# First stage of a mixture-of-experts kernel: five channel groups of 24 rows in place of four of 32, variance by VectorE, normalisation on GpSimd inside the channel loop, x handed on per image group

## The reference, cut to what matters

```
m = mean(x, channels);  v = var(x, channels);  y = (x - m) / sqrt(v + eps)
weight[c, kh, kw] = codebook[hash(c, kh, kw)] * sign(c, kh, kw)
x1[n, c] = x[n, c] + sum over kh, kw of weight[c, kh, kw] * y[n, c, h + kh - 3, w + kw - 3] + bias[c]
```

## Time and profile before

| what | us |
|---|---|
| median of three runs | 1649.24 |
| span of the profiled execution (the page gives no other time of it) | 1726.5 |
| VectorE starts on x | 7.57 |
| first product of the convolution | 80.06 |
| last step of the convolution on VectorE | 215.06 |
| routing stage's first loads | 255.22 |
| first scatter | 273.52 |
| last scatter of the routing stage | 530.21 |

### The profile page before, as it was taken

How to read it: one execution, slowest core, us unless ns; L and a number is a source line. 1 busy time by engine, 2 the same in 40 slices (tenths; PEclk the granted TensorE clock), 3 DMA queues, 4 the chain that set the end, 5 groups by cost and what they waited for, 6 DMA issues and landing times. The chain is left out here.

```text
span 1726.5 us, 31708 instructions
## 1 busy us (share of the span) xinstructions
PE 1207.4 (70%) x6568; PEld 956.4 (55%) x6569; DVE 1106.1 (64%) x4125; ACT 587.5 (34%) x1099; POOL 699.3 (41%) x680
## 2 busy tenths in 40 slices
PE   4799903223222999999946979889797089999940
PEld 4799902212122999998934545455454067777730
DVE  7677704434345666666648688787876467777754
ACT  4233303323231444444432234334344134444320
POOL 0100005565574444444434045345554535555530
PEclk9899955555555999999976989989898589999975
DMA  4033297121111222222232011121011122222239
GB/s 200 22 107 106 64 121 273 53 58 55 39 44 46 66 62 62 62 63 60 62 128 79 1 46 51 28 58 42 26 32 31 40 73 74 75 79 71 73 103 261
DMA packets 139200, 129.26 MB, mean 75 GB/s; under 512 B 56291, under 2 KB 119012, under 8 KB 138214
## 3 DMA queue, kind: packets, MB, share of 16 engines
q1 hardware_dynamic: 89396, 79.76, 16.9%
q0 software_dynamic: 19968, 39.44, 7.0%
q10 hardware_dynamic: 29778, 9.45, 2.7%
HBM read 78.66 MB, written 50.99 MB: 75 GB/s over the span
## 5 line engine op out<-in xcount | busy, mean ns | idle before, releaser
L594 POOL DMA_INDIRECT routed<-r_xn,r_slot x320 | 333.3, 1042 | 346.6 <-DVEq L583 233.9
L823 POOL DMA_INDIRECT answers<-e_y,e_dest x304 | 291.1, 958 | 347.1 <-ACT e_y L922 272.9
L972 DVE COPY e_ht<-e_ps_ht 128x512 f32<-128x512 f32 (+1 forms) x304 | 169.5, 558 | 180.9 <-PE e_ps_ht L859 156.7
L867 PE MATMUL e_ps_y<-w,e_ht 128*128 x1824 | 258.6, 278 | 13.4 <-DVE e_ht L972 7.4
L867 PEld LDWEIGHTS e_ps_y<-w,e_ht 128*128 128x128 f32 x1824 | 228.6, 192 | 20.1 <-issue 18.8
L1135 PE MATMUL c_pz<-c_c,down 116*120 116x512 f32 (+1 forms) x392 | 199.7, 627 | 0.0
L922 ACT ACTIVATE e_y<-e_ps_y,e_weight 128x128 f32<-128x128 f32 x304 | 111.8, 368 | 217.7 <-issue 117.9
L859 PE MATMUL e_ps_ht<-ident,e_h 128*128 128x128 f32 x912 | 150.8, 274 | 6.0 <-DVE e_h L958 5.5
L849 PE MATMUL e_ps_h<-w1h,e_xl 128*128 x308 | 150.9, 490 | 1.1 <-issue 0.7
L1109 PE MATMUL c_py<-c_xh,gl 121*116 121x512 f32 (+1 forms) x196 | 124.1, 633 | 39.1 <-DVE c_xl L1215 27.1
L859 PEld LDWEIGHTS e_ps_ht<-ident,e_h 128*128 128x128 f32 x912 | 115.4, 141 | 56.0 <-DVE e_h L958 10.7
(11 more groups left out here) (134 smaller groups left out, 2445.4 us busy)
## 6 DMA issues: line engine op xcount, KB each, us to landing
e_xg<-routed SPq DMA_DIRECT2D x318, 66.0 KB
answers<-answers SPq DMA_DIRECT2D x32, 480.0 KB
c_w<-in_w SPq DMA_DIRECT2D x32, 448.0 KB
c_x<-in_xh SPq DMA_DIRECT2D x4, 1536.0 KB
routed<-r_xn,r_slot POOLq DMA_INDIRECT x320
answers<-e_y,e_dest POOLq DMA_INDIRECT x304
x<-x SPq DMA_DIRECT2D x96, 48.0 KB
w1l<-in_w SPq DMA_DIRECT2D x2, 2048.0 KB, 10.3
```

Source lines behind the costliest of these rows:

```text
L594: ro.nc.gpsimd.indirect_dma_start(ro.xs, bass.IndirectOffsetOnAxis(ap=ro.slot[0:px, q, c:c + 1], axis=0), ro.xn[0:px, q, k, t, :], None).t ...
L823: nc.gpsimd.indirect_dma_start(ys, bass.IndirectOffsetOnAxis(ap=dest[:, s:s + 1], axis=0), y[:, s, :], None).then_inc(stored[s], 16)
L867: ins = nc.tensor.matmul(ps_y[s % 2][:, 0:P], ht[:, s % 2, c * P:(c + 1) * P], wt.w2[:, bass.ds(w + c * P, P)], start=c == 0, stop=c == ch ...
L972: nc.vector.tensor_copy(ht[:, s % 2, :], ps_ht[s % 2][:, 0:HID]).then_inc(ht_ready, 1)
```

## The change

Five groups of 26 channel indices stand on 5 x 24 = 120 partitions (CP), with no blank rows; the last group has 24 real channels and two of zeros. The columns are now ordered by image group, image column and image (of four), and so are the padded buffers. The number of channel indices falls from 32 to 26. The matrices are 120 x 120.

The mean is subtracted into a buffer `cen` of the layout of x, one instruction per quarter. ScalarE squares into `sq`, which now uses the memory of `r.x`; VectorE sums the squares over the channels and one small product per quarter adds over the groups. The inversion is done once for all 384 columns. The normalisation itself is done by GpSimd for one channel at a time into a ring of three padded buffers, inside the loop. Signs and bias are applied by ScalarE on the accumulator (two instructions), and VectorE adds the result to x. Loops of this stage are written out.

The first constants of the routing stage are loaded at the start of the first one. x stays on the chip past the first stage; the routing stage stores it in four DMAs, one per image group, and loads a tile by one DMA per image row and channel group once the group's store has landed.

```diff
-CGS, CIN, RPAD = 4, 32, 32
+CGS, CIN = 5, 26
+CP = CGS * SIDE
+LAST_CIN = P - CIN * (CGS - 1)
+LAST_P = (CGS - 1) * SIDE
...
+            for i in range(CIN):
+                if i >= NRING:
+                    pool.wait_ge(split_ready, i - NRING + 1)
+                nc.gpsimd.tensor_tensor(nrm[0:CP, i % NRING, :, HALO:HALO + SIDE, :].rearrange("p g w t -> p g (w t)"),
+                                        cen[0:CP, :, i].rearrange("p (g n) -> p g n", g=IMAGE_GROUPS),
+                                        rstd[0:CP, :].rearrange("p (g n) -> p g n", g=IMAGE_GROUPS), ALU.mult).then_inc(normed, 1)
...
+            def square(q):
+                act.wait_ge(centred, q + 1)
+                nc.scalar.activation(sq[0:CP, quarter(q), 0:LAST_CIN], cen[0:CP, quarter(q), 0:LAST_CIN], ACT.Square)
+                nc.scalar.activation(sq[0:LAST_P, quarter(q), LAST_CIN:CIN], cen[0:LAST_P, quarter(q), LAST_CIN:CIN], ACT.Square
+                                     ).then_inc(squared, 1)
+
+            def high_w(i):
+                act.wait_ge(w_in[i % WRING], 16 * (i // WRING + 1))
+                if i >= 2:
+                    act.wait_ge(acc_ready, i - 1)
+                nc.scalar.activation(wh[0:CP, i % 2], wring[0:CP, i % WRING], ACT.Copy).then_inc(wh_ready, 1)
+
+            def high_x(i):
+                act.wait_ge(normed, i + 1)
+                nc.scalar.activation(ph[0:CP, i % 2], nrm[0:CP, i % NRING], ACT.Copy).then_inc(ph_ready, 1)
+
+            def scale_out(i):
+                act.wait_ge(acc_ready, i + 1)
+                acc = ps[i % 4][0:CP, 0:NW].rearrange("p (a b t) -> p a b t", b=2, t=IG)
+                for odd in range(2):
+                    ins = nc.scalar.activation(acc[:, :, odd, :], acc[:, :, odd, :], ACT.Identity, bias=bias[0:CP, i:i + 1],
+                                               scale=osign[0:CP, (i + odd) % 2:(i + odd) % 2 + 1])
+                ins.then_inc(scaled, 1)
...
+            for i in range(CIN):
+                if i + 1 < CIN:
+                    if i + 1 >= 2:
+                        high_w(i + 1)
+                    high_x(i + 1)
+                if i:
+                    scale_out(i - 1)
+            scale_out(CIN - 1)
...
             def variance(q):
-                pe.wait_ge(squared, q + 1)
-                for c in range(CIN):
-
-                    ins = nc.tensor.matmul(ps_stat[q][:, 0:Q], mean_w[:], sq[:, q * Q:(q + 1) * Q, c], start=c == 0, stop=c == CIN - 1)
-                ins.then_inc(var_summed, 1)
+                pe.wait_ge(var_summed, q + 1)
+                nc.tensor.matmul(ps_stat[q][0:CP, Q:2 * Q], mean_w[0:CP], part[0:CP, quarter(q)], start=True, stop=True
+                                 ).then_inc(var_ready, 1)
...
+            def low_w(i):
+                dve.wait_ge(wh_ready, i + 1)
+                nc.vector.tensor_tensor(wl[0:CP, i % 2], wring[0:CP, i % WRING], wh[0:CP, i % 2].bitcast(F32), ALU.subtract
+                                        ).then_inc(w_free, 1)
...
+            def add_out(i):
+                dve.wait_ge(scaled, i + 1)
+                nc.vector.tensor_tensor(x[0:CP, :, i], ps[i % 4][0:CP, 0:NW], x[0:CP, :, i], ALU.add).then_inc(acc_free, 1)
...
+            for ig in range(IMAGE_GROUPS):
+                sp.dma_start(x1d[ig].rearrange("p w t c -> p (w t) c"), c0_x[0:CP, ig * SIDE * IG:(ig + 1) * SIDE * IG, :]
+                             ).then_inc(x_out[ig], 16)
+
             def load(ig, q):
-                px = pixels(q)
-
-                need(sp, ro.norm.applied, QT * (ig - 1) + q + 1)
-                for row in range(px // SIDE):
-                    sp.dma_start(r.x[row * SIDE:(row + 1) * SIDE, bass.ds(QT * ig + q, 1)].rearrange("p a t c -> p (a t) c"),
-                                 src[ROWS * q + row].rearrange("(n w) c -> w n c", w=SIDE)[:, bass.ds(IG * ig, IG), :]
-                                 ).then_inc(x_in[q], 16)
+                if q == 0:
+                    sp.wait_ge(x_out[ig], 16)
+                if ig:
+                    sp.wait_ge(ro.norm.applied, QT * (ig - 1) + q + 1)
+                for row in range(pixels(q) // SIDE):
+                    for cg in range(CGS):
+                        cw = CIN if cg < CGS - 1 else LAST_CIN
+                        sp.dma_start(r.x[row * SIDE:(row + 1) * SIDE, QT * ig + q, :, cg * CIN:cg * CIN + cw],
+                                     x1d[ig, cg * SIDE + ROWS * q + row, :, :, 0:cw]).then_inc(x_in[q], 16)
```

More of the change, by code:

```diff
@@ L168, in conv0_phase @@
+        x_in = [sem(f"c0_x_in{i}") for i in range(4)]
         w_in = [sem(f"c0_w_in{i}") for i in range(WRING)]
[L169 to L172, removed]
@@ L174, in conv0_phase @@
         Q = NW // 4
-        PER_STORE = 8
+        quarter = lambda q: slice(q * Q, (q + 1) * Q)
         block = ctx.enter_context(nc.Block())
[L178 to L187, removed]
@@ L191, in _ @@
             for q in range(4):
[L192 to L200, removed]
@@ new lines, in variance @@
+                nc.tensor.matmul(ps_stat[q][0:CP, Q:2 * Q], mean_w[0:CP], part[0:CP, quarter(q)], start=True, stop=True
+                                 ).then_inc(var_ready, 1)
+            for q in range(4):
+                mean(q)
+                if q >= 2:
+                    variance(q - 2)
+            variance(2)
+            variance(3)
+            for i in range(CIN):
+                h = i % 2
+                pe.wait_ge(split_ready, i + 1)
+                if i >= 4:
+                    pe.wait_ge(acc_free, i - 3)
+                parts = ((wh, ph), (wl, ph), (wh, pl))
+                for n in range(3 * TAPS):
+                    kw, (w, v) = n // 3, parts[n % 3]
+                    ins = nc.tensor.matmul(ps[i % 4][0:CP, 0:NW], w[0:CP, h, kw * CP:(kw + 1) * CP], v[0:CP, h, :, kw:kw + SIDE, :].rearrange("p g w t -> p g (w t)"),
+                                           start=n == 0, stop=n == 3 * TAPS - 1)
+                ins.then_inc(acc_ready, 1)
@@ L328, in turn @@
-            def turn(it, last):
-                step = Chain(dve, chain, base + 2 * WRING * it)
-                for s in range(WRING):
-                    i = WRING * it + s
-                    if not (last and s == WRING - 1):
-                        split(i + 1, s + 1)
-                    dve.wait_ge(acc_ready, i + 3)
-                    step.after(nc.vector.scalar_tensor_tensor(tmp[:, s % 2, :], ps[s][:, 0:NW], osign[:, s % 2:s % 2 + 1],
-                                                              check[:, 1, :], ALU.mult, ALU.mult))
-                    dve.sem_inc(acc_free, 1)
-                    xr = x[:, :, bass.ds(i, 1)].rearrange("p n a -> p (n a)")
-                    step.after(nc.vector.scalar_tensor_tensor(xr, tmp[:, s % 2, :], bias[:, bass.ds(i, 1)], xr, ALU.add, ALU.add))
-                    dve.sem_inc(x1_ready, 1)
@@ L349 @@
+            low_w(0)
+            low_w(1)
+            low_x(0)
+            for i in range(CIN):
+                if i + 1 < CIN:
+                    if i + 1 >= 2:
+                        low_w(i + 1)
+                    low_x(i + 1)
+                if i:
+                    add_out(i - 1)
+            add_out(CIN - 1)
+            dve.wait_ge(acc_free, CIN)
+            dve.wait_ge(before_ready, 1)
 class Routing:
@@ L683, in load_weights @@
                 weights_load(wt, sp, io, 0, w_in)
-            groups(sp, load, load_weights)
-            sp.wait_ge(blank_in, 16)
+            for q in range(QT):
+                load(0, q)
+            load_weights()
+            for ig in range(1, IMAGE_GROUPS):
+                for q in range(QT):
+                    load(ig, q)
             route_store_tails(ro, sp)
```

250 lines of the change are left out of this document (110 added, 140 removed).

## The result

The changed kernel takes **1773.29 us** (1773.17 to 1777.76, four runs) against 1648.05 beside it: a ratio of 1.0773 [1.0753, 1.0793], 7.7% slower where 1577 was forecast. The first stage became as short as the forecast said, a little shorter. The loss stands behind it, in the loads of x.

The account below looks back on a forecast made before the run. It took TensorE to bound the channel loop and GpSimd's scatters to pace the routing stage. Saving 95.4 and losing 20 or 27 gave -75 or -68, taken as -72: 1649.2 - 72 = 1577 us, range 1555 to 1630.

Parts of the forecast that it names:

- (c): Passing x to the routing stage: 480 loads issued 0.42 us apart, first scatter at 38, 20 us lost, 27 without pauses.
- Rival 2: Routing stage: slower than before if an SP issue costs over 0.69 us, or 0.58 without pauses; 1705 or 1780; chance 0.06.
- Its 0.96: Routing loads: us per issue for seven held issues of 24; at that price the stage is 502, net +130.
- (a): Statistics and normalisation in the first stage: first convolution product near 49 (46 to 60) instead of 80.06, 31 us less.
- the 6 allowed: Start of the routing stage: about 6 us until the first store of 1.2 MB has landed, scaled by size.
- (b): Convolution's channel loop: TensorE stays the bound, 25 channels at 4.05 us after a first of 5.4, sum 106.7.
- Rival 1: Routing stage: SP's issues, 0.578 us each, are the pace; net -52 to -2, 1597 to 1647; chance 0.17.
- Rival 4: Routing stage: slower tile arrival removes VectorE's pauses, which timed runs do have; stage 253, not 276; 1531; chance 0.07.
- Rival 3: Channel loop: VectorE and GpSimd block one another, chain 2.8 becomes 4.7, 17 us more; 1594; chance 0.08.
- The order of releases: Channel loop: GpSimd's product starts after the low x part, ends before the next pair; blocking put at nothing.
- the 63 thought possible: Routing stage: ten pauses of some 6.3 us, possibly 63 of the profiled execution's 77 us over the median.

Follow-up runs that it names:

- e4: Changed kernel with the same 480 loads, each written as one run of 416 bytes per partition (values differ from the reference's); 1675.89 us.
- e18: Changed kernel with 16 bytes of padding behind each pixel's four images in DRAM, round without pauses; 1612.63 us against 1650.36, ratio 0.9784.
- e7: Changed kernel storing x as rows of 128 channels (20 stores, 96 loads), with x and weights loaded as 128 partitions; 1662.28 us, ratio 0.9657.
- e11: Changed kernel with each product's moving operand read as 16 runs of 24, not 4 of 96 (values differ from the reference's); 1787.65 us.
- e17: Changed kernel, unchanged, run again in a round with pauses; 1819.32 us against 1741.03 for the kernel before, ratio 1.0477.
- e16: The kernel of e10, unchanged, in a round with pauses; 1658.08 us against 1741.03 for the kernel before, ratio 0.9539.
- e10: e7 with group 0's stores on two queues and later stores and weights queued behind loads needed first; 1565.51 us against 1649.93, ratio 0.9484.
- e3: Changed kernel with four loads per image row instead of five, pieces of 128 bytes from a contiguous source (values differ from the reference's); 1742.12 us.
- e2: Kernel before, with each routing-stage load cut in five, 480 in all, from rows of 128 channels; 1802.49 us against 1732.17.

## Why the prediction was wrong

**The step that failed: (c), "I take 0.42".** The forecast let a load cost 376 ns to issue and 0.42 us from one to the next. It was 784 and 0.87. All else follows: tile 1's first work at 211.82, first scatter 62.3 us after the stage's start where 38 was forecast, then 21 us per tile where GpSimd needs 10.4. Rival 2 had the mechanism, the threshold (0.58 without pauses) and the formula: 480 issues and 41 us more, at 0.87 that is 459 for the stage, and 457 were measured from first store to last scatter. What it had wrong was the chance, 0.06, and the reason. Its 0.96 came from seven issues held beside a large copy, which I could explain away, and rightly: traffic is not what makes 784, since e4 and e18 issue as many loads beside the same scatters at 365 and 376. That 0.96 lies near 0.87 is luck. But the row of 376 ns was for another pair of shapes, four pieces of 512 bytes per partition into one run. The kernel before has no row for a load whose source pieces lie at one even distance and whose destination is strips, so 0.42 was the nearest row and not a bound; (a) kept both ends for its uncertain rates, and (c) went on with one number.

**How far the rest stands.** With the issue price back at 376 (e18), 1612.63, the outcome lies inside 1555 to 1630 and 36 over 1577. Half of the 36 stands at the first scatter: 215.92 against 197.8 forecast (159.8 + 38), because the padded stores take 14.6 more than the 6 allowed and 50 issues at 0.51 take 4.5 more than at 0.42, less 3 of earlier start. The other half is the pace behind it: 233.5 us from first to last scatter against 214 forecast (207 + 7).

**(a) Right in its mechanism, 7 us off.** Forecast 49, measured 55.97, inside 46 to 60. The reductions (2.71 forecast) and the subtractions (2.8) took 2.75 and 2.74: the fast rate held for a contiguous output. Six of the 7 us are the loads: the first quarter at 9.36 for 7.3, and waits of 3.23 and 1.41 for the next two, where 0.5 was allowed. I scaled the load's time by its bytes, and these loads of 120 partitions move at half the rate. With 128 partitions (e7) the first product starts at 48.9. The rest is VectorE's first low part, 1.67 us instead of 0.65 beside GpSimd's first products.

**(b) Right in the bound, period too long.** 3.69 for 4.05, so 25 channels are 9 us shorter. I took the weight loads' 192 ns as their own length and as the pace. e11 shows the step that was wrong: with 16 runs the loads are 184 and still come 0.193 apart, held by the products, and these get cheaper with 96 elements in a run. By luck this made up for (a): the stores start at 156.81, forecast with all signals 159.8.

**Rival 1** is out, as issues came 0.87 apart and not 0.578. **Rival 4** is out too: the slow loads did leave room for the pauses (e17), as it said, but the timed runs didn't have them, and the loads cost more than any pause. **Rival 3** happened only before the loop: in it L319's median is 650 ns. The order of releases kept GpSimd's 1.23 us product clear of both low parts, as the step in (b) said.

**The profiled execution.** That its 77 us over the median were partly the pauses was right, some 44 for the 63 thought possible. Since timed runs and trace were of unlike rounds, the spans of before and after (1726.5 and 1771.4) show +45 where the runs show +125.

**Open.** Why some rounds pause after every 8 or 16 scatters was not settled. GpSimd is not where the pauses begin: in e16's stage VectorE stands still 33.7 us in seven waits before L544 and ScalarE 44.0 in five before L563, whose end the trace puts down to no instruction of this core, and e10's trace of the same kernel has no such wait. Nor is it settled what in the issue takes the 400 ns more: the trace shows only its length.

## What to carry over

An issue's price on a queue is a number of its own: with hundreds of small DMAs per stage, find a row with the same source and destination shapes, or carry both ends into the chances. When a queue's DMAs come slower than their bytes explain, look at the issue's duration and the DMA share first, and try a few bytes of padding, or put the cutting into the stores. A transfer of 120 partitions and an operand in short runs each have a price too: pad to 128, and put the longest run innermost.

## What the hardware showed

- One issue on SP, 24 pixels x 4 images each: source pieces at one even distance and destination in strips 784 ns (104 and 128 bytes, touching or 8 bytes apart: change and e3); source of 24 runs of 416 bytes, 16 bytes apart, into the same strips 376 (e18); source of 96 pieces, images far apart, into the same strips 375 (e2, group 0); one run into 24 runs of 416 bytes 365 (e4).
- Loads of 120 partitions: 214 GB/s at a DMA share of 0.99; of 128 partitions 424 at 1.03 (e7).
- Products with 384 columns in 16 runs of 24 cost some 17 ns more than in 4 runs of 96.
- Stores of 4.8 MB from SBUF: in runs of 416 bytes 20.6 us until the first of four had landed, in runs of 9984 bytes 7.2; in 46080 pieces of 104 bytes 86 us for the whole, 1.9 ns a piece.
- The same kernel takes 1648 to 1650 us in some rounds and 1720 to 1741 in others; with what it changes is open.
